# Attention stage of an attention and feed-forward kernel: one of a step's two query blocks is transposed by VectorE and carried by SBUF transfers

## The reference

```python
qkv = (x @ Wqkv + bqkv).reshape(B, S, 3, H, Dh)
kwin = jnp.concatenate([kp[:, :, :-2], kp[:, :, 1:-1], kp[:, :, 2:]], axis=3)
scores = jnp.einsum('bhnqd,bhnkd->bhnqk', qb, kwin) * scale
mask = (jnp.abs(kpos - qpos) <= W) & (kpos >= 0) & (kpos < S)
attn = jax.nn.softmax(jnp.where(mask[None, None], scores, jnp.float32(-1e+30)), axis=-1)
out = jnp.einsum('bhnqk,bhnkd->bhnqd', attn, vwin)
return out @ Wout + bout
```

## Time and profile before

| | |
|---|---|
| median of 3 runs | 2626.13 us (2625.84 to 2630.6) |
| profiled execution, whole time | 2629.41 us |
| its span | 2627.6 us |
| mean granted clock of TensorE | 0.989 of 2.4 GHz |
| busy share of the span | PE 98%, ScalarE 62%, VectorE 61%, GpSimd 24% |

### The profile page before, as it was taken

How to read it: one execution, slowest core, us unless ns; L and a number is a source line. 1 busy time by engine, 2 the same in 40 slices (tenths; PEclk the granted TensorE clock), 3 DMA queues, 4 the chain that set the end, 5 groups by cost and what they waited for, 6 DMA issues and landing times.

```text
span 2627.6 us, 55989 instructions
## 1 busy us (share of the span) xinstructions
PE 2576.2 (98%) x19728; PEld 2090.2 (80%) x19728; DVE 1592.0 (61%) x4779; ACT 1638.1 (62%) x4260; POOL 631.8 (24%) x595
## 2 busy tenths in 40 slices
PE   6999999999999999989999999999999999999998
PEld 4888888888888888868888888888888888888885
DVE  5444444444444444357777777777777777777775
ACT  6333333333333333358888888888888888888886
POOL 0011111111111111033333333333333333333332
PEclk7999999999999999999999999999999999999999
DMA  5422222222222222021121111112111111112110
GB/s 181 146 80 81 80 80 80 80 80 80 80 80 80 80 80 64 33 81 34 34 65 34 53 46 42 58 41 58 34 61 39 42 58 42 58 34 65 34 46 29
DMA packets 188361, 167.43 MB, mean 64 GB/s; under 512 B 11328, under 2 KB 143424, under 8 KB 187632
## 3 DMA queue, kind: packets, MB, share of 16 engines
q1 hardware_dynamic: 188000, 164.41, 20.2%
q0 software_dynamic: 144, 0.17, 0.0%
HBM read 97.43 MB, written 67.11 MB: 63 GB/s over the span
## 4 chain that ended last, share of the span: by engine, by line
PE 55%; ACT 1%; issue 0%; DVE 0%; POOL 0%; POOLq 0%; ACTq 0%
PE pT_ps L1193 14%; PE job_ps L1105 14%; PE score_ps L1176 7%; PE job_ps L1123 7%; PE job_ps L1217 7%; PE job_ps L1114 7%; ACT wqkv_raw L928 1%; ACT wqkv_raw L938 0%; PE job_ps L1237 0%; PE score_ps L1227 0%; DVE wqkv_raw L1006 0%; DVE k_lo L1038 0%; ACT q_hi L954 0%; ACT k_hi L957 0%; POOL wout_raw L899 0%
## 5 line engine op out<-in xcount | busy, mean ns | idle before, releaser
L928 ACT ACTIVATE wqkv_raw<-wqkv_raw,neg_max 128x384 f32<-128x384 f32 (+1 forms) x1024 | 633.3, 619 | 186.3 <-DVE neg_max L1006 181.5
L888 POOL TENSOR_SCALAR wqkv_raw<-wqkv_raw,sum_rcp 128x384 f32<-128x384 f32 (+1 forms) x256 | 372.9, 1457 | 960.1 <-DVE sum_rcp L1017 960.1
L494 ACT ACTIVATE relu<-up_ps,fc_scale 128x512 f32<-128x512 f32 x256 | 176.2, 688 | 656.2 <-PE up_ps L625 656.2
L938 ACT COPY wqkv_raw<-pT_ps 128x384 f32<-128x384 f32 (+1 forms) x1024 | 484.7, 474 | 74.4 <-PE pT_ps L1193 74.1
L1193 PE MATMUL pT_ps<-ident,wqkv_raw 128*128 128x128 f32 x3040 | 513.4, 277 | 8.1 <-ACT wqkv_raw L938 7.7
L1006 DVE CUSTOM_DVE_ANT_0 wqkv_raw<-score_ps,mask 128x384 f32<-128x384 f32 (+1 forms) x1024 | 503.5, 548 | 5.7 <-PE score_ps L1176 1.6
L568 DVE SCALAR_TENSOR_TENSOR sq<-up_ps,relu 128x512 f32<-128x512 f32 x256 | 177.0, 692 | 531.8 <-ACT relu L494 530.4
L1193 PEld LDWEIGHTS pT_ps<-ident,wqkv_raw 128*128 128x128 f32 x3040 | 360.0, 140 | 119.1 <-ACT wqkv_raw L938 42.6
L635 PE MATMUL down_ps<-proj_T,sq_hi 128*128 128x512 f32 x1024 | 408.9, 399 | 0.9 <-DVE sq_lo L551 0.9
L637 PE MATMUL down_ps<-proj_T,sq_lo 128*128 128x512 f32 x1024 | 404.3, 395 | 0.0
L621 PE MATMUL up_ps<-f_xT_hi,fc_T 128*128 128x512 f32 x1024 | 399.2, 390 | 1.4 <-DVE low L539 1.4
(11 more groups left out here) (126 smaller groups left out, 4228.2 us busy)
## 6 DMA issues: line engine op xcount, KB each, us to landing
xT_hi<-xT SPq DMA_DIRECT2D x65, 256.0 KB, 3.8
xT_lo<-xT SPq DMA_DIRECT2D x65, 256.0 KB, 4.5
f_x_in<-in_L_attn_x SPq DMA_DIRECT2D x64, 256.0 KB, 3.2
xT<-f_xT_hi SPq DMA_DIRECT2D x64, 256.0 KB, 2.6
xT<-f_xT_lo SPq DMA_DIRECT2D x64, 256.0 KB, 2.8
part_in<-in_L_attn_x SPq DMA_DIRECT2D x64, 256.0 KB, 3.4
partial<-f_y SPq DMA_DIRECT2D x64, 256.0 KB, 2.0
wout_raw<-partial SPq DMA_DIRECT2D x64, 256.0 KB, 2.8
```

The lines of the kernel that those rows point to most:

```text
L888: nc.gpsimd.tensor_scalar(probs[:, u, cols], probs[:, u, cols], sum_rcp[:, u:u + 1], None, ALU.mult).then_inc(last_head_normalised, 1)
L928: nc.scalar.activation(probs[:, u, cols], probs[:, u, cols], ACT.Exp, bias=neg_max[:, u:u + 1], scale=-1.0, accum_out=prob_sum[:, u:u + 1] ...
L938: nc.scalar.copy(pT[:, h, first + seen.start:first + seen.stop, :].rearrange("p w t -> p (w t)"), pT_ps[:, h % 2, seen.start * P:seen.stop ...
```

## The change

Block 1 of a step stays as it was. Block 0 no longer passes through TensorE and PSUM:

- its four heads are normalised by ScalarE (heads 0 and 1, `normalise_first_heads`) and by VectorE (heads 2 and 3, `normalise_first_unit`); GpSimd now does one head a step instead of two;
- VectorE transposes each head in blocks of 32x32 (`turn_blocks`, four instructions a step on 128x384) into `blocks`;
- SP issues sixteen SBUF-to-SBUF transfers a step (`move_blocks`), each from 32 partitions to 32 others, 3 runs of 512 bytes a partition (48 KB), into `pT_moved`; each of the four semaphores `blocks_moved` counts four of them;
- turn_probs and copy_pT of block 0 are gone (12 transposes and 4 copies a step);
- probs_times_values now goes by block, 48 recorded matmuls of 128 columns instead of 32 of 256 and 128;
- the ring of values has 5 slots instead of 6, and oT_hi and oT_lo are rings of 6 steps; SP's loop runs over steps, with the other transfers behind the moves of their step.

The core of the diff:

```diff
+            def move_blocks(t):
+                i, _ = where(t)
+                seen = blocks_seen(i, 0)
+                sp.wait_ge(blocks_turned, HC * (t + 1))
+                if t >= 1:
+                    sp.wait_ge(pv_done, t)
+                for strip in range(STRIPS):
+                    for place in range(STRIPS):
+                        sp.dma_start(pT_moved[place * DH:(place + 1) * DH, seen.start:seen.stop, strip, :, :],
+                                     blocks[strip * DH:(strip + 1) * DH, seen.start:seen.stop, place, :, :]
+                                     ).then_inc(blocks_moved[strip], 16)
...
+            def normalise_first_heads(t):
+                i, _ = where(t)
+                cols = window(i, 0)
+                act.wait_ge(rcp_done, 4 * t + 1)
+                for u in range(HC // 2):
+                    nc.scalar.mul(probs[:, u, cols], probs[:, u, cols], sum_rcp[:, u:u + 1]
+                                  ).then_inc(act_heads_normalised, 1)
...
                 for h in range(HC):
                     if 1 <= t <= STEPS:
-                        copy_pT(t - 1, 1, h)
+                        copy_pT(t - 1, h)
                     if t < STEPS:
                         exp(t, 0, h)
+                if t < STEPS:
+                    normalise_first_heads(t)
...
                     if h == 0 and 1 <= t <= STEPS:
                         oT_high(t - 1)
-                    if t < STEPS:
-                        copy_pT(t, 0, h)
...
+            def turn_blocks(t, u):
+                i, _ = where(t)
+                seen = blocks_seen(i, 0)
+                if u < HC // 2:
+                    dve.wait_ge(act_heads_normalised, HC // 2 * t + u + 1)
+                else:
+                    dve.wait_ge(dve_heads_normalised, HC // 2 * (t - 1) + u + 1)
+                if u == HC // 2 and t >= 1:
+                    for moved in blocks_moved:
+                        dve.wait_ge(moved, 16 * STRIPS * t)
+                nc.vector.transpose(blocks[:, seen.start:seen.stop, :, u, :].rearrange("p w a t -> p (w a) t"),
+                                    probs[:, u, seen.start * P:seen.stop * P].rearrange("p (b t) -> p b t", t=DH)
+                                    ).then_inc(blocks_turned, 1)
...
                     find_max(t, 0)
-                    normalise(t, 0)
+                    for pair in range(2):
+                        inverse_sums(t, 0, pair)
+                    normalise_first_unit(t)
+                    for u in (2, 3, 0, 1):
+                        turn_blocks(t, u)
...
                 if 1 <= t <= STEPS:
                     probs_times_values(t - 1)
                 for part in range(QUARTERS):
-                    if t < STEPS:
-                        turn_probs(t, 0, part)
                     run_b(t, part)
```

More of the change, by code:

```diff
@@ L725, in attention_stage @@
         normalised, last_head_normalised = sem("normalised"), sem("last_head_normalised")
+        act_heads_normalised, dve_heads_normalised = sem("act_heads_normalised"), sem("dve_heads_normalised")
+        blocks_turned = sem("blocks_turned")
+        blocks_moved = [sem(f"blocks_moved{q}") for q in range(STRIPS)]
         turned = sem("turned")
@@ L856, in _ @@
                 load_part(0, b)
[L857 to L863, removed]
+            for t in range(STEPS + DC):
+                i, c = where(t)
+                if t < STEPS:
+                    move_blocks(t)
+                if c == 1 and i + XR - 1 < NT:
                     load_x(i + XR - 1)
+                if c >= 2 and i >= 1:
+                    store_y(i - 1, c - 2)
+                    if i < NT:
+                        load_part(i, c - 2)
             for b in range(2):
@@ L943, in oT_high @@
                 act.wait_ge(pv_done, t + 1)
[L944 to L946 removed]
+                if i >= 1 and c == OR - DC:
+                    act.wait_ge(job_filled, B_NUMBER[4 * i + 2])
+                nc.scalar.copy(oT_hi[:, t % OR, :], job_ps[:, pv_bank(t), 0:T]).then_inc(oT_hi_done, 1)
             def qk_high(u, number, bank):
@@ L1001, in find_max @@
                 dve.wait_ge(scored, 2 * t + b + 1)
-                if t >= 1:
-                    dve.wait_ge(turned, 8 * (t - 1) + HC * (b + 1))
+                if t >= 1 and b == 0:
+                    dve.wait_ge(blocks_turned, HC * t)
+                if t >= 1 and b == 1:
+                    dve.wait_ge(turned, HC * t)
                 for h in range(HC):
@@ L1008, in find_max, with inverse_sums @@
                                                    accum_out=neg_max[:, u:u + 1]).then_inc(maxed, 1)
-            def normalise(t, b):
-                i, _ = where(t)
[L1012 to L1022, removed]
+            def inverse_sums(t, b, pair):
+                first = b * HC + 2 * pair
+                heads = slice(first, first + 2)
+                dve.wait_ge(exped, 8 * t + first + 2)
+                nc.vector.reciprocal(sum_rcp[:, heads], prob_sum[:, heads]).then_inc(rcp_done, 1)
@@ new lines, in normalise @@
+            def normalise(t, pair):
+                i, _ = where(t)
+                cols = window(i, 1)
+                first = HC + 2 * pair
+                inverse_sums(t, 1, pair)
+                dve.wait_ge(rcp_done, 4 * t + 2 + pair + 1)
+                for u in range(first, first + 2):
+                    if u % HC < HC - 1:
+                        nc.vector.tensor_scalar(probs[:, u, cols], probs[:, u, cols], sum_rcp[:, u:u + 1], None,
+                                                ALU.mult).then_inc(normalised, 1)
@@ new lines, in normalise_first_unit @@
+            def normalise_first_unit(t):
+                i, _ = where(t)
+                cols = window(i, 0)
+                dve.wait_ge(rcp_done, 4 * t + 2)
+                for u in range(HC // 2, HC):
+                    nc.vector.tensor_scalar(probs[:, u, cols], probs[:, u, cols], sum_rcp[:, u:u + 1], None, ALU.mult
+                                            ).then_inc(dve_heads_normalised, 1)
+            def turn_blocks(t, u):
+                i, _ = where(t)
+                seen = blocks_seen(i, 0)
[9 more added lines that the diff above has]
+                                    ).then_inc(blocks_turned, 1)
@@ L1082, in _ @@
                 if t < STEPS:
-                    normalise(t, 1)
+                    for pair in range(2):
+                        normalise(t, pair)
             add_out(NT - 1, 1, B_NUMBER[STEPS + 2], b_bank(STEPS + 2))
@@ L1256, in _ @@
                     if 1 <= t <= STEPS:
-                        turn_probs(t - 1, 1, part)
+                        turn_probs(t - 1, part)
                     run_a(t, part)
```

90 lines of the change are left out of this document (46 added, 44 removed).

## The result

The changed kernel takes 3062.8 us (median of four runs, 3055.2 to 3069.3) beside 2626.7 for the kernel before: ratio 1.166 (95% interval 1.162 to 1.169), 436 us more, where 2800 was predicted. A step takes 14.85 us for 11.44 (11.44 + 436/128). The profiled execution has a span of 3065.4 us.

A forecast was written before the change was run, and what follows sets the result against it. TensorE was taken as the bound before, the VectorE and ScalarE chain after: 10.45 + 4 x 0.50 = 12.45 us, plus 0.35 for the clock, 12.80 against 11.44 over 128 steps, +174 us, so 2800 us; range 2675 to 2970.

The forecast's parts named there:

- The sign: Whole kernel: slower than before, with chance 0.87; faster 0.10, same 0.03.
- TensorE's part: TensorE, attention stage: loses 12 transposes, 1.32 us a step, and then needs 10.1 to 10.4 us a step.
- The formula 10.45 + 4X: Step time of the VectorE and ScalarE chain after the change, with X one VectorE transpose; 12.45 us at X = 0.50.
- F to G: From the start of find_max of block 0 to that of block 1: 6.19 + 4X us.
- G to the next F: From the start of find_max of block 1 to that of the next block 0: 4.26 us.
- X: Price of one VectorE transpose of 128x384: taken as 0.50 us, ends 0.375 and 0.90.
- Heads 0 and 1 at nothing: ScalarE's two multiplications cost nothing on the chain, covered by VectorE's work; at most 1.2 us without that cover.
- The clock: TensorE at 1.2 GHz after idling between run_b and the next scores, in half the steps: +0.35 us, ends 0 and 1.0.
- The transfers at nothing: SP's sixteen transfers a step: their loop of 11.1 us stays hidden under the step of 12.8 us.
- I = 0.43: Issue time of one transfer on SP, 0.43 us from a load of 128 runs; sixteen make 6.9 us a step.
- The wait for pv_done at nothing: SP's wait ahead of the transfers costs nothing, because the product with the values ends before the transposes do.
- The first rival: SP's transfers bound the kernel: issue 0.61 us by access shape, loop 14.0 us, +328 us, 2954 us; chance 0.20.

The follow-up runs named there:

- the other order: Changed kernel without its transfers, VectorE turning heads 0 and 1 at once, then qk_low, heads 2 and 3 behind find_max of block 1: 2529.9 us, ratio 0.962.
- the kernel filled ahead of run_b: Changed kernel without its transfers, TensorE given sixteen unread identity transposes between the product with the values and run_b: 2726.1 us, ratio 1.036.
- the filling: Sixteen unread TensorE transposes: ahead of run_b in the changed kernel without transfers, 2726.1 us; ahead of the product in the changed kernel with transfers, 3019.4 us.
- the long runs: Changed kernel with blocks and pT_moved laid out so each of the sixteen transfers has 32 runs of 1536 bytes for 96 of 512: 3031.2 us, ratio 1.153.
- the kernels through DRAM: Changed kernel with blocks stored to DRAM and loaded back: five transfers, 2877.4 us; with heads 2 and 3 turned behind find_max of block 1, 2760.5; that in halves, 2784.4.

## Why the prediction missed

The sign and the first mechanism held; the size did not. The 436 us by the runs: the chain at full clock 2726 - 2626 = 100 (predicted 129), the clock 2891 - 2726 = 165 (predicted 45), the transfers 3063 - 2891 = 172 (predicted 0). The last two overlap: taken in the other order, with the clock held first, the transfers are 293 and the clock 44. Either way the transfers, put at nothing, are the largest miss.

- *TensorE's part*, 10.1 to 10.4 us a step: right. Where the other order let it run, it was busy 484.4 of 500 us at 10.68 us a step, 10.35; that is the upper end, with the sixteen instructions more counted.
- *The formula 10.45 + 4X*: right to 0.1 us once the clock is out of it (12.33 for 12.22), and in both of its parts. In the kernel filled ahead of run_b, F to G is 7.97 us on the mean of 90 steps, where 6.19 + 4 x 0.47 is 8.07, and G to the next F is 4.24, where 4.26 was worked out.
- *X*: taken 0.50; four in 1.96 us, 0.47 from start to start. The plain row, find_max's 0.49, was the better guide than the 0.58 worked out beside it. The Trainium skill's rule that a whole 128x128 turn belongs on TensorE where PSUM will do (VectorE: DVE Perf Modes, "Rules for kernel authors") came out true of this kernel, ratio 1.166, though the transposes themselves are its smallest cost, 106 us at full clock.
- *Heads 0 and 1 at nothing*: right here, since the transposes cover them. Without that cover they are on the path, 1.01 us of the 1.2 named.
- *The clock*, +0.35: the mis-sized term, and placed wrongly. From G to the next F the kernel without transfers takes 5.37 us on the mean of 90 steps, for the 4.26 of the prediction and the 4.24 that the filling brought back; F to G is 8.17. The prediction saw one idle piece, between run_b and the next scores. It missed that run_b takes over a PSUM bank that qk_low reads, and that qk_low was being moved 1.9 us later on VectorE: that makes an idle piece ahead of run_b, whose own twelve matmuls then run mostly at 1.2 GHz and push out the next find_max. The 1.0 kept as the upper end was also short. And the forecast didn't carry it: X = 0.58 with the clock at 1.0 gives 10.45 + 2.32 + 1.0 = 13.8 us, 2924, not the "about 13.0", 2826, that is named as its end.
- *The transfers at nothing*: the step that failed, and in it the term I = 0.43, the issue time by the number of runs. A transfer measured 0.60 us median, and 0.67 from one to the next on the mean, since the next starts 0.64 us after the last and four in a hundred take 1.3 us on the mean. So 16I is 10.8 us and not 6.9, and the prediction's own loop, 4X + 16I + 2.1 + 0.1, is then 1.9 + 10.8 + 2.2 = 14.9, where 14.85 was measured. By its own test, that the transfers decide from I = 0.54 on, it was over the line.
- *The wait for pv_done at nothing* ("the product ends before the transposes do"): wrong too, but small. It reads the product's place from the kernel before; in the changed kernel the product itself waits for the landing, as the transposes do, and where it runs at 1.2 GHz its 2.8 us end later than their 1.96. That was so in 59 of 100 steps, and worth 0.44 us a step, 56 us of the whole by this count; the filling, which took it away, brought 44.
- *The first rival* (issue 0.61, loop 14.0, 2954) had the right mechanism with a chance of 0.20. Its 0.61 was right for one issue; it left out the 0.06 us between them and the long ones, 1.0 us in sixteen. Its ground, three dimensions for two, is refuted by the long runs, so its 0.61 is in part luck. The range to 2970 was built from cases that each had one cause.
- *What would show it*: TensorE under 85% (80), stretches at 0.50 and transposes of 0.5 us came true. "With no wait for a transfer" did not, 180 us in 89 steps, and VectorE at 66% instead of near 80 said the same: the step was longer than its chain. Without transfers and at full clock VectorE stands at 78%. An issue time above 0.54 us was named as what would make the prediction wrong, and it did.

## To carry to other kernels

Before work is put into an engine's queue, list what stands behind it there and what each of those releases, buffers and PSUM banks included: here the read of a bank, moved by 1.9 us, cost 165 us through TensorE's clock, where the inserted transposes by themselves cost 106. Count small transfers in issues of one queue, not in bytes, and follow each loop right round, through landing and the consumer that frees the destination. Where two loops are nearly as long, opening one of them gains little or nothing: look in the trace how often each is the later. When a transfer is put between two engines, the consumer's place in the step is no longer that of the trace before.

## What was not expected of the hardware

- Sixteen SBUF to SBUF transfers of 48 KB occupy SP's queue for 10.2 to 11.9 us, 10.8 on the mean; one issue takes 0.59 to 0.60 us median with 96 runs of 512 bytes or 32 of 1536. The store of 512 runs to DRAM takes 0.34 median, each load back 0.43. What sets the 0.60 stays open.
- The same store of y is issued in 0.34 us (median) in the kernel before and in the one without transfers, in 0.59 behind the sixteen, and in 0.43 in the kernels through DRAM; the issue time of a transfer isn't its own alone.
- One idle piece of 1.9 us in a step of 13.5 was followed by 1.2 GHz in most of run_b, a microsecond after TensorE had begun to work again. Sixteen transposes that nobody reads, 1.96 us, in its place kept 2.4 GHz for the 500 us looked at. Put behind run_b they left the idle piece as it was, 1.9 us in every step, and still the mean clock rose from 0.925 to 0.979. Which idle time brings the low clock isn't settled by these runs.
